# A graph-attention layer: the slope branch of 896 columns of each unit formed by TensorE in PSUM and taken in by one VectorE pass

## The reference, cut to what matters

```python
# layer 0: N = 4096 nodes, 256 features, 4 heads of 64, ALPHA = -0.2
h = inputs @ W
hr = h.reshape(N, F_OUT, H)
s_src = jnp.einsum('nfh,fh->nh', hr, a[:F_OUT])
s_dst = jnp.einsum('nfh,fh->nh', hr, a[F_OUT:])
e = s_src[:, None, :] + s_dst[None, :, :]
e = jnp.where(e >= 0, e, ALPHA * e)
att = jax.nn.softmax(e * adj[:, :, None], axis=1)
out = jnp.einsum('ijh,jfh->ihf', att, hr)
out = out.reshape(N, H * F_OUT) + bias + inputs @ res_w + res_b
x = layernorm(x + out)
```

## Time and profile before

| | us |
|---|---|
| median of 3 runs | 3946.87 (3944.33 to 3949.57) |
| the profiled execution: its time | 3949.58 |
| the profiled execution: its span | 3947.7 |
| TensorE busy (matmul) | 3601.9 (91%) |
| VectorE busy | 3572.2 (90%) |
| ScalarE busy | 3065.4 (78%) |
| GpSimd busy | 1337.5 (34%) |

### The profile page before, as it was taken

How to read it: one execution, slowest core, us unless ns; L and a number is a source line. 1 busy time by engine, 2 the same in 40 slices (tenths; PEclk the granted TensorE clock), 3 DMA queues, 4 the chain that set the end, 5 groups by cost and what they waited for, 6 DMA issues and landing times.

```text
span 3947.7 us, 66296 instructions
## 1 busy us (share of the span) xinstructions
PE 3601.9 (91%) x25368; PEld 3037.3 (77%) x25368; DVE 3572.2 (90%) x6240; ACT 3065.4 (78%) x3107; POOL 1337.5 (34%) x1508
## 2 busy tenths in 40 slices
PE   8888888888888859999999989999999999999993
PEld 5777777777777748787777768888887888888883
DVE  4999999999999969999999499999999899999994
ACT  6999999999999955555555378888888788888870
POOL 0000000000000001111111155555655569999996
PEclk9999999999999989999999999999999999999996
DMA  2112112112112140000000333333333433333331
GB/s 107 51 56 83 56 56 83 56 56 83 56 56 83 56 133 15 17 17 17 21 17 19 116 92 97 99 100 97 96 101 105 132 114 119 119 115 116 114 101 42
DMA packets 155870, 302.98 MB, mean 77 GB/s; under 512 B 16666, under 2 KB 117274, under 8 KB 151298
## 3 DMA queue, kind: packets, MB, share of 16 engines
q1 hardware_dynamic: 155522, 298.49, 23.6%
HBM read 256.67 MB, written 41.75 MB: 76 GB/s over the span
## 4 chain that ended last, share of the span: by engine, by line
DVE 50%; PE 21%; ACT 16%; POOL 7%; issue 4%; DMA 1%; DVEq 0%; SPq 0%; ACTq 0%; POOLq 0%; PEldq 0%; PEld 0%
DVE b L1344 12%; DVE b L1342 12%; PE ps L872 8%; PE ps L945 6%; DVE b L1395 4%; ACT b L1191 4%; ACT b L1192 4%; DVE b L1562 3%; DVE b L1340 3%; DVE b L1453 3%; DVE b L1451 3%; DVE b L1432 2%; POOL b L584 2%; ACT b L1172 2%; POOL b L581 2%
## 5 line engine op out<-in xcount | busy, mean ns | idle before, releaser
L872 PE MATMUL ps<-b 128*128 128x257 f32 x4096 | 911.6, 382 | 21.1 <-DMA b<-in_adjTb 11.9
L945 PE MATMUL ps<-b 128*128 128x257 f32 x4096 | 903.1, 380 | 0.0
L872 PEld LDWEIGHTS ps<-b 128*128 128x128 f32 x4096 | 776.8, 190 | 146.7 <-DMA b<-in_adjTb 13.2
L945 PEld LDWEIGHTS ps<-b 128*128 128x128 f32 x4096 | 772.0, 190 | 113.4 <-ACT b L1129 0.8
L806 PE MATMUL ps<-cb,b 128*128 128x128 f32 x4096 | 507.0, 280 | 199.6 <-ACT b L1019 161.2
L806 PEld LDWEIGHTS ps<-cb,b 128*128 128x128 f32 x4096 | 456.5, 144 | 248.7 <-ACT b L1019 184.1
L1342 DVE SCALAR_TENSOR_TENSOR b<-b 128x4096 f32<-128x4096 f32 x128 | 566.5, 4426 | 13.4 <-ACT b L1013 9.1
L1344 DVE CUSTOM_DVE_ANT_0 b<-b 128x4096 f32<-128x4096 f32 x128 | 566.4, 4425 | 4.4
L547 POOL TENSOR_TENSOR cb<-cb 128x1 f32<-128x1 f32 x32 | 39.4, 1232 | 1395.0 <-DVE cb L1324 1395.0
L1026 ACT ACTIVATE b<-ps 128x1024 f32<-128x1024 f32 x512 | 490.9, 1063 | 9.5 <-PE ps L806 9.4
L1019 ACT ACTIVATE b<-b 128x4096 f32<-128x4096 f32 x128 | 482.0, 3766 | 3.7 <-DVE b L1346 3.1
(11 more groups left out here) (194 smaller groups left out, 4899.1 us busy)
## 6 DMA issues: line engine op xcount, KB each, us to landing
b<-in_adjTb SPq DMA_DIRECT2D x256, 512.0 KB, 3.8
b<-in_adj SPq DMA_DIRECT2D x32, 2048.0 KB, 8.5
h_d<-b SPq DMA_DIRECT2D x64, 128.0 KB, 1.8
b<-h_d SPq DMA_DIRECT2D x64, 128.0 KB, 2.6
b<-in_xT SPq DMA_DIRECT2D x4, 1024.0 KB, 9.7
b<-in_xT SPq DMA_DIRECT2D x32, 128.0 KB, 8.3
gx_d<-b SPq DMA_DIRECT2D x32, 128.0 KB, 1.8
X_d<-b SPq DMA_DIRECT2D x32, 128.0 KB, 8.3
```

Of the source, the lines that this page charges most:

```text
L872: last = mm(b[:, 0:XA], aj[:, q % AJR, e, :], xf[:, j, :], start=(j == 0), stop=(j == NT - 1))
L945: last = mm(o[:, 0:XA], at[:, q % ATR, b, :], xa[:, j, :], start=(j == 0), stop=(j == NT - 1))
```

## The change

For the units from EU = 3 on, columns 0 to 895 (EC) no longer get a sum of their own in SBUF.

- TensorE forms -0.2 (s_src + s_dst) of these columns in a PSUM slot, with two float32r products (512 and 384 columns) of four rows (`slopes`): two rows of the left factor `eL` are ones and meet the two parts of -0.2 s_dst in `eR`; two hold the parts of -0.2 s_src and meet ones. The four heads lie at partitions 0, 32, 64 and 96.
- VectorE adds and compares in one pass: the larger of (s_dst + s_src) and the PSUM value. It does so behind the slope pass, which now covers columns 896 to 4095.
- VectorE's own sum now covers columns 896 to 1791, ScalarE's 1792 to 4095 (LA).
- The `slopes` of unit u + 2 are issued in unit u, behind the fourth turn (and `turn_x`) and ahead of the second pv. They take a slot of the ring; that slot comes free when VectorE has read it (`s_ea`).
- The ring `pt` has 3 buffers in place of 4, and the first pv of a unit now stands between its third and its fourth turn.
- At the start, `WD` has four more columns in each half (-0.2 s_src, -0.2 s_dst), VectorE fills `eR` and `eL` with ones and scales the new columns, and GpSimd issues DMAs: the two parts of -0.2 s_dst into `eR`, the two of -0.2 s_src into a DRAM tensor, and from there, two DMAs for each tile, two tiles ahead, into `eL`. `xtl`, `u10` and `WA` are moved in SBUF.

```diff
-    PTR = 4
+    PTR = 3
+    EC = 896
+    LA = EC + 896
+    EU = 3
...
-        WD = p0.take(2, 40)
+        WD = p0.take(2, 44)
...
             for u in range(NU):
...
+            if EU <= u + 2 < NU:
+                ring.append(("e", u + 2))
...
@@ gpsimd
+            def factors(t):
+                w = slice(t % 2 * 128, t % 2 * 128 + 128)
+                for i in range(2):
+                    po.dma_start(rows_of(eL[:, w], 2 + i), el_d[i][:, t * 128:(t + 1) * 128]).then_inc(s_el[t % 2], 16)
+            po.wait_ge(s_lo, NL)
+            po.wait_ge(s_e1, 1)
+            for i in range(2):
+                p = 32 * i
+                po.dma_start(rows_of(eR, i), hr[p + 4:p + 8, 0:EC]).then_inc(s_er, 16)
+                po.dma_start(el_d[i], hr[p + 8:p + 12, :]).then_inc(s_els, 16)
+            po.wait_ge(s_els, 16 * 2)
+            for t in range(2):
+                factors(t)
             for tt in range(NT):
+                if tt + 2 < NT:
+                    po.wait_ge(s_ef, 4 * (tt + 1) - EU)
+                    factors(tt + 2)
                 po.wait_ge(s_ve, tt + 1)
@@ tensor
-            def slot0(i):
+            def slot0(kind, j):
+                i = place[kind, j]
                 if i >= 3:
-                    pe.wait_ge(s_ev, i - 2)
+                    before = ring[i - 3]
+                    pe.wait_ge(s_ea if before[0] == "e" else s_ev, order[before] + 1)
                 return bank(2 * (i % 3), 2)
+            def slopes(u):
+                t, h = divmod(u, 4)
+                pe.wait_ge(s_el[t % 2], 32 * (t // 2 + 1))
+                b = slot0("e", u)
+                p = slice(32 * h, 32 * h + 4)
+                for lo in range(0, EC, 512):
+                    hi = min(lo + 512, EC)
+                    last = mm(b[:, lo:hi], eL[p, t % 2 * 128:t % 2 * 128 + 128], eR[p, lo:hi],
+                              start=True, stop=True)
+                last.then_inc(s_ef, 1)
...
-                for c in range(NCH):
+                for c in range(3):
                     turn(g0 + c)
+                pv(g0)
+                turn(g0 + 3)
                 if u % 4 == 0 and u >= 8:
                     turn_x((u - 8) // 4)
-                pv(g0)
+                if EU <= u + 2 < NU:
+                    slopes(u + 2)
                 pv(g0 + 1)
@@ scalar
-                act(ub[:, u % UB, LSP:N], sd_s[:, h, LSP:N], ACT.Identity,
+                lo = LSP if u < EU else LA
+                act(ub[:, u % UB, lo:N], sd_s[:, h, lo:N], ACT.Identity,
                     bias=ssc[:, t, h:h + 1]).then_inc(s_e, 1)
@@ vector
+            one_s = sd_s[:, 0, 0:EC]
+            link(v.memset(one_s, 1.0))
+            v.tensor_copy(eL[:, :], one_s[:, 0:256])
+            v.tensor_copy(eR[:, :], one_s).then_inc(s_e1, 1)
...
-            v.tensor_copy(WD[:, :, 0:4], dst)
-            last = v.tensor_copy(WD[:, :, 32:36], dst)
+            for p in (0, 32):
+                v.tensor_copy(WD[:, :, p:p + 4], dst)
+                v.tensor_scalar(WD[:, :, p + 4:p + 8], dst, SLOPE, None, ALU.mult)
+                last = v.tensor_scalar(WD[:, :, p + 8:p + 12], src, SLOPE, None, ALU.mult)
...
-                link(v.tensor_scalar(b[:, 0:LSP], sd_s[:, h, 0:LSP], ssc[:, t, h:h + 1], None, ALU.add))
+                sc = ssc[:, t, h:h + 1]
+                lo, hi = (0, LSP) if u < EU else (EC, LA)
+                link(v.tensor_scalar(b[:, lo:hi], sd_s[:, h, lo:hi], sc, None, ALU.add))
                 ve.wait_ge(s_e, u + 1)
-                link(v.scalar_tensor_tensor(out=b, in0=b, scalar=SLOPE, in1=b, op0=ALU.mult, op1=ALU.max))
+                last = v.scalar_tensor_tensor(out=b[:, lo:N], in0=b[:, lo:N], scalar=SLOPE, in1=b[:, lo:N],
+                                              op0=ALU.mult, op1=ALU.max)
+                if u >= EU:
+                    link(last)
+                    ve.wait_ge(s_ef, u - EU + 1)
+                    last = v.scalar_tensor_tensor(out=b[:, 0:EC], in0=sd_s[:, h, 0:EC], scalar=sc,
+                                                  in1=slot_bank("e", u, 2)[:, 0:EC], op0=ALU.add, op1=ALU.max)
+                    last.then_inc(s_ea, 1)
+                    ve.wait_ge(s_ea, u - EU + 1)
+                else:
+                    link(last)
```

More of the change, by code:

```diff
@@ L91, in gat_topp_kernel @@
             pass
-        YS, HR = 152, 39064
+        YS, HR = 152, 38808
+        ER = HR + 3 * N + 784
         with nc.sbuf_tensor("pad0", [128, YS], F32), nc.sbuf_tensor("selR", [128, 512], F32R) as selR, \
                 nc.sbuf_tensor("pad1", [128, HR - YS - 512], F32), nc.sbuf_tensor("hr", [128, N], F32R) as hr:
+            pass
+        with nc.sbuf_tensor("pad2", [128, ER], F32), nc.sbuf_tensor("eR", [128, EC], F32R) as eR, \
+                nc.sbuf_tensor("eL", [128, 256], F32R) as eL:
             pass
@@ L130, in gat_topp_kernel @@
         pt = r0.take(PTR, TBK, 128)
+        u10 = r0.take(2, 512)
+        p0 = Region(b0, r0.at)
+        WA = p0.take(2, 264)
         xts = r0.take(2, 128)
+        xtl = r0.take(2, 128)
+        r0.at = p0.at
         mkq0 = r0.take(2, 128)
-        u10 = r0.take(2, 512)
+        assert r0.at == ER
+        r0.take(EC + 256)
         selF = ots
         xT_s = b0[:, HR + N:HR + 3 * N].rearrange("p (k n) -> p k n", k=2)
-        p0 = Region(b0, r0.at - 1024)
-        WA = p0.take(2, 264)
         p0 = Region(b0, HR - 4 * N)
@@ L243, in gat_topp_kernel @@
         s_yv = sem("s_yv")
+        s_e1 = sem("s_e1")
+        s_er = sem("s_er")
+        s_els = sem("s_els")
+        s_el = [sem(f"s_el{i}") for i in range(2)]
+        s_ef = sem("s_ef")
+        s_ea = sem("s_ea")
         s_ms = sem("s_ms")
@@ L296, in gat_topp_kernel, with slot_bank @@
         groups[2 * NL] = tuple(range(3 * NL + 1, NT))
[L298 to L301, removed]
+        ring = []
         for u in range(NU):
             if u % 4 == 1 and u >= 9:
-                gslot[(u - 9) // 4] = i
-                i += 1
+                ring.append(("g", (u - 9) // 4))
             for c in range(NCH):
-                slot_of[u * NCH + c] = i
-                i += 1
+                ring.append(("p", u * NCH + c))
             if u % 4 == 0 and u >= 8:
-                xslot[(u - 8) // 4] = i
-                i += 1
+                ring.append(("x", (u - 8) // 4))
+            if EU <= u + 2 < NU:
+                ring.append(("e", u + 2))
         for t in range(NGX, NT):
-            xslot[t] = i
-            i += 1
+            ring.append(("x", t))
+        place, order = {}, {}
+        for i, (kind, j) in enumerate(ring):
+            place[kind, j] = i
+            order[kind, j] = sum(1 for k, _ in ring[:i] if (k == "e") == (kind == "e"))
+        slot_of = {j: order["p", j] for k, j in ring if k == "p"}
+        xslot = {j: order["x", j] for k, j in ring if k == "x"}
+        gslot = {j: order["g", j] for k, j in ring if k == "g"}
+        def slot_bank(kind, j, n=1):
+            return bank(2 * (place[kind, j] % 3), n)
         def turned(u):
@@ L321, in gat_topp_kernel @@
             g = {}
-            for n in ("kk", "kq", "ks", "pl", "el", "mx", "xp", "mask", "av", "R", "rv", "pz", "gx",
-                      "gd", "po", "rd", "xs", "acc", "nz", "hi", "gi", "yd", "ys", "fi", "fa", "s1", "f1", "s2",
-                      "fo", "fd", "lv", "lr", "lt", "e8", "bt", "bf", "xc", "tp"):
+            names = ("kk", "pl", "el", "mx", "xp", "mask", "av", "rv", "pz", "po", "xs", "acc", "nz", "lv")
+            if s == 0:
+                names += ("kq", "ks", "gx", "gd", "lr", "xc")
+            else:
+                names += ("R", "rd", "hi", "gi", "yd", "ys", "fi", "fa", "s1", "f1", "s2", "fo", "fd", "lt", "e8", "bt",
+                          "bf", "tp")
+            for n in names:
                 g[n] = sem(f"{n}_{s}")
@@ L544, in _, with rows_of @@
             nc.gpsimd.memset(mhalf, -0.5).then_inc(s_ms, 1)
+            def rows_of(tile, r):
+                return tile[r:r + 97:32, :]
+            def factors(t):
[11 more added lines that the diff above has]
+                factors(t)
             for tt in range(NT):
+                if tt + 2 < NT:
+                    po.wait_ge(s_ef, 4 * (tt + 1) - EU)
+                    factors(tt + 2)
                 po.wait_ge(s_ve, tt + 1)
@@ L704, in _ @@
                 for k in range(2):
-                    last = mm(bank(1 + c % 2)[0:40, :], WD[:, k, :], xT_s[:, k, c * 512:(c + 1) * 512],
+                    last = mm(bank(1 + c % 2)[0:44, :], WD[:, k, :], xT_s[:, k, c * 512:(c + 1) * 512],
                               start=(k == 0), stop=(k == 1))
@@ L746, in _ @@
             pe.wait_ge(s_mc, 1)
+            pe.wait_ge(s_er, 16 * 2)
             def pv(gq):
@@ L1025, in ev @@
                     ac.wait_ge(s_pv, gq - PTR + 1)
-                act(pt[:, gq % PTR].rearrange("p a b -> p (a b)"), bank(2 * (i % 3), 2)[:, 0:CW],
+                act(pt[:, gq % PTR].rearrange("p a b -> p (a b)"), slot_bank("p", gq, 2)[:, 0:CW],
```

(8 more changed lines are left out.)

25 lines of the change are left out of this document (16 added, 9 removed).

## The result

The changed kernel takes 4003.36 us (4002.65 to 4004.8) where the kernel before takes 3947.68 us in the same comparison: ratio 1.0142, 95% interval 1.0130 to 1.0154. The profiled execution has a span of 4003.0 us against 3947.7, 55.3 more.

A forecast was written before the change was run, and what follows sets the result against it. VectorE was taken as the bound at 42.41 us a round, passing to the ScalarE-TensorE chain at 43.66. Thirty rounds x 1.61 = 48.3, less 10.7, plus the ends, gave +42 us: 3989 us, range 3955 to 4006.

The forecast's parts named there:

- The bound: Layer 0 rounds: VectorE bounds at 42.41 us, ScalarE's chain through TensorE takes 42.05; the change passes the bound to that chain.
- VectorE's part: VectorE's three passes in a unit: sum -0.33, slope pass -0.93, new pass +1.18, together -0.08 us; a round of 42.1 us.
- ScalarE's part: ScalarE's sum in each unit has 256 columns fewer: -0.22 us.
- TensorE's part: TensorE, by heads: `slopes` 0.60 us, a pv 0.95; heads 2 and 3 +0.24 each, head 0 -0.17, head 1 +1.3.
- the pv ahead of the fourth turn: First pv of a unit on TensorE, 0.95 us: the fourth copy in heads 2 and 3 starts 0.46 us later.
- The ring: `pt` with 3 buffers: the fourth copy waits for the first pv, done before the fourth turn anyway; cost nothing.
- The clock: TensorE's granted clock taken at 0.99, the 2.4 GHz level; `slopes` reach 1.22 us only if it falls.
- The ends: Outside the rounds: first two and last two units +3.8 us, units 2 to 6 +0.8, VectorE's setup instructions +0.3.
- VectorE stays the bound: Rival: the chain grows under 0.06 us a round, so 9.5 us are won: 3937 us; chance 0.12.
- the third pass is dear: Rival: VectorE's PSUM pass at double time per column, +3.4 us a round, 4042 us; chance 0.03.
- Half the loss: Rival: the head-1 stretch of TensorE has unseen play, so 0.8 us a round, +18 us: 3965 us; chance 0.07.

The follow-up runs named there:

- run 6: Kernel before, with `rows` issued behind the fourth turn of head 1 and its copies behind the exponential of head 2: 3948.91 us, ratio 1.0002.
- run 7: Kernel before, with `rows` moved behind the fourth turn of head 1 and VectorE's sum cut from 1536 to 1152 columns: 3933.23 us, ratio 0.9961.
- the control: Kernel before, with only VectorE's part of the sum cut from 1536 to 1152 columns and nothing moved: 3977.64 us, ratio 1.0073.
- run 5: Changed kernel, with VectorE's third pass 64 columns wide in place of 896: 4362.45 us, only layer 0 comparable, round 43.92 us against 43.94.
- run 1: Kernel before, with only the first pv of a unit put between its third and fourth turn, ring of four: 4010.96 us, ratio 1.0166.
- run 2: Kernel before, order untouched, with the ring `pt` of three buffers in place of four: 4010.49 us, ratio 1.0162.
- run 3: Changed kernel, with the first pv put back behind the fourth turn and `turn_x`, ring of three: 4002.11 us, ratio 1.0141.
- run 4: Changed kernel, with the two products of `slopes` 64 columns wide each in place of 512 and 384: 3992.9 us, ratio 1.0115.
- run 8: Changed kernel, with `rows` moved behind the fourth turn of head 1 and its copies behind the exponential of head 2: 3961.97 us, ratio 1.0033.
- run 9: Changed kernel, with `rows` moved behind the fourth turn of head 1 and SyncE's stores of its results one tile later: 3959.88 us, ratio 1.0032.
- run 11: Changed kernel, with the DMAs of `eR` and `eL` issued by SyncE in place of GpSimd: 3997.71 us, ratio 1.0123.

## Why the prediction was right

The forecast was 3989 us, the range 3955 to 4006, and 4003.36 lies in its upper end: the bound passed where it was said to pass, and most of the terms that were too small or missing add up in one direction.

*The bound.* Right. The chain was 42.05 us a round and VectorE's 42.41, and runs 6, 7 and the control measure both from outside: shortening the chain alone wins nothing, moving columns from VectorE to ScalarE alone loses 28 us, both together win 15.

*VectorE's part.* Right. The three passes are within 10 ns of the sum (0.68, 3.49, 1.14 us), so that a round of VectorE's own work would be 42.1 us. The Trainium skill ("VectorE: DVE Perf Modes", the errata section) has 62 more fixed cycles, 0.065 us, for a PSUM source, by which the saving would have been 0.02 us a unit, an estimate from the page. The rows don't show them. 1148 ns are 933 for 896 columns and 215 fixed, and a pass of layer 1 that also takes its scalar from memory but reads SBUF alone has more: 4492 - 4267 = 225 fixed, by the page of the profile of the kernel before.

```profile
L1562 DVE SCALAR_TENSOR_TENSOR b<-b 128x4096 f32<-128x4096 f32 x64 | 287.5, 4492 | 42.9 <-issue 30.9
```

The saving was real and never showed in the time, as VectorE's waits and run 5 say.

*ScalarE's part.* Right: the sum takes 2459 - 2217 = 242 ns less, where 0.22 us were taken.

*TensorE's part.* Right in kind, 0.28 us a round too small. `slopes` cost 607.77 - 607.20 = 0.57 us at the place where they count, in front of `turn_back` and `rows`, where 0.60 was taken. The mis-sized term is the pv ahead of the fourth turn: "A pv costs (637.93 - 636.03) / 2 = 0.95 us". That was half of a pair of pv that follow each other. Between a turn and a turn it takes 619.93 - 618.90 = 1.03, 0.08 more. At each such change of work the weight loads stand still for 0.17 us (PEld at 618.90); that this is the reason was not tested. The difference is 0.08 in each of heads 2 and 3 and 0.15 in head 1. Heads measured 10.21, 13.85, 9.95 and 9.95 for 10.19, 13.7, 9.87 and 9.87.

*The ring.* The prediction put the new place of the pv down as the cause and the ring at nothing: "for the fourth copy that is the first pv, which is done before the fourth turn anyway". This holds for the order as written, but not as an account of the cause. Either alone is enough: the order in run 1, the ring of three in run 2; and with the ring of three, undoing the order gives nothing back (run 3). That both stood in the change and cost only once is why the number came out.

*The clock.* The sum was made at 0.99, and the clock was 1.00. That is partly luck: the prediction did not look at what a longer wait does to the clock, and the same new order cost 14 us by a lower clock in run 1, where no `slopes` fill TensorE's gap.

*The ends.* The start cost 4.3 us up to unit 7, some 3 expected. The barrier's 2.7 us are a term that the prediction put at nothing: the prediction followed GpSimd's queue through the rounds and stopped there. With 8.5 us of the rounds (46.1 for 37.6), 1.3 of the start, 2.7 of the barrier and 1.9 of layer 1, less 1.2 of the 1.5 us taken for the last two units, this is the 13 us between the 42 forecast and the 55 measured.

*The rivals.* "VectorE stays the bound" falls by run 5, "the third pass is dear" by that run and by the 1148 ns. "Half the loss" falls by the heads: there was no play in the stretch.

## What to carry to other kernels

Where two engines are both nearly full, write down both rounds, with the waits of each, and ask of every edit what it does to the second one; here 0.4 us a round separated them, and the change gave 0.3 to one and took 1.9 from the other. The price of a moved memory is its buffers: here a ring that is one shorter was a wait in every unit, and it cost the same wherever the waiting work was written. Work that comes once a round belongs where the engine has a gap; here only with that done did a shift of columns between the engines pay.

## What the runs showed of the hardware

- TensorE's clock: with the order changed (run 1), TensorE is idle for 2.03 us in front of the turns in the ordinary units, and in 12 of 116 units the next three turns run mostly at the 1.2 GHz level and take 4.50 us instead of 2.84. With the ring changed (run 2) the idle time is 2.25 us and 14 units are hit. The kernel before has it too, in six places (behind gaps of 2.08 to 2.10 us), which is why its clock is 0.99 in the earlier trace rows; run 6, with gaps up to 2.89 us, has 18 in its rounds, and they cost nothing there, since VectorE sets its round. The changed kernel with gaps of 1.44 us, run 4 with 1.70 and the control of run 7 with 1.71 show none in their rounds. In runs 1 and 2 a stall that let TensorE rest cost more than its own length.
- GpSimd in a barrier after DMAs of its own: the barrier opened 4.06 us after ScalarE's last copy (4.31 in runs 3, 8 and 9), in place of 1.33 in run 11 and in the kernel before. That it is the drain of its queue is inferred from the releaser and from run 11.
- A pv between two turns costs TensorE 1.03 us, and 0.95 as half of a pair of pv, so that a change between the two kinds of work costs some 0.08 us. It goes with 0.17 us in which the weight loads stand still; what causes them is not shown.
